# One key tile fewer summed on GpSimd: six of eight by additions, the last two by the ones product

## The reference

```python
result = embeddings @ w_qkv                       # 16 heads of 32
q, k, v = ...                                     # each (b, heads, s, 32)
scores = jnp.einsum('bnqd,bnkd->bnqk', q, k) / jnp.sqrt(jnp.float32(h))
probs = jax.nn.softmax(scores, axis=-1)
ctx = jnp.einsum('bnqk,bnkd->bnqd', probs, v)
...
x = _layernorm(x + attention(x))
x = _layernorm(x + ffn(x))
```

## Time and profile before

| | before |
|---|---|
| median of 3 runs | 4126.71 us (4125.9 to 4129.7) |
| the profiled execution, whole | 4124.68 us |
| its span, first to last instruction | 4123.0 us |
| PE busy | 3806.5 us, 92% |
| DVE busy | 3051.1 us, 74% |
| POOL busy | 2283.0 us, 55% |
| ACT busy | 1749.4 us, 42% |
| granted TensorE clock, mean | 0.977 |

### The profile page before, as it was taken

How to read it: one execution, slowest core, us unless ns; L and a number is a source line. 1 busy time by engine, 2 the same in 40 slices (tenths; PEclk the granted TensorE clock), 3 DMA queues, 4 the chain that set the end, 5 groups by cost and what they waited for, 6 DMA issues and landing times. The chain is left out here.

```text
span 4123.0 us, 61806 instructions
## 1 busy us (share of the span) xinstructions
PE 3806.5 (92%) x22985; PEld 1728.9 (42%) x22985; DVE 3051.1 (74%) x4929; ACT 1749.4 (42%) x3104; POOL 2283.0 (55%) x1446
## 2 busy tenths in 40 slices
PE   3489999999999999999999999999999999999999
PEld 2234344433543345433453434443454334534344
DVE  8866687676876778666786668776786667866787
ACT  3345522664235632455225552265423553245522
POOL 4468722885239832588227862298424883268722
PEclk9689999999999999999999999999999999999999
DMA  4110110111010110111101101101101111010110
GB/s 163 44 58 26 29 50 24 35 32 50 23 35 18 40 44 24 30 32 32 47 19 40 29 21 54 31 22 32 53 22 32 26 34 48 19 37 24 32 49 21
DMA packets 106560, 152.56 MB, mean 37 GB/s; under 512 B 28177, under 2 KB 55569, under 8 KB 106129
## 3 DMA queue, kind: packets, MB, share of 16 engines
q1 hardware_dynamic: 106256, 148.49, 11.6%
HBM read 76.28 MB, written 19.66 MB: 23 GB/s over the span
## 5 line engine op out<-in xcount | busy, mean ns | idle before, releaser
L571 DVE TENSOR_REDUCE mx<-R 128x1 f32<-128x512 f32 x2080 | 1334.4, 686 | 662.6 <-PE R L663 654.6
L1186 ACT ACTIVATE arena<-SC 128x512 f32<-128x512 f32 x1344 | 749.7, 603 | 413.9 <-PE SC L1438 411.0
L1512 PE MATMUL SC<-wgu,split 128*128 128x512 f16 (+1 forms) x3456 | 724.0, 364 | 0.6
L1084 POOL TENSOR_TENSOR wd<-wd,arena 128x1024 f32<-128x1024 f32 x208 | 485.7, 2357 | 31.0 <-ACT arena L1186 29.9
L1110 POOL TENSOR_TENSOR arena<-arena,sc_h 128x704 f32<-128x704 bf16 (+2 forms) x136 | 176.1, 1312 | 576.8 <-DVE arena L496 576.8
L1186 ACT ACTIVATE wd<-SC 128x512 f32<-128x512 f32 x704 | 399.8, 603 | 201.1 <-PE SC L1438 196.9
L1512 PEld LDWEIGHTS SC<-wgu,split 128*128 128x128 f16 x3456 | 338.3, 98 | 343.8 <-issue 12.6
L663 PE MATMUL R<-ks_even,qs_even 96*128 96x512 bf16 x1056 | 398.5, 399 | 88.6 <-issue 45.3
L1227 ACT ACTIVATE arena<-SC,gain 128x512 f32<-128x512 f32 (+1 forms) x192 | 125.1, 652 | 775.0 <-PE R L1512 390.7
L643 PE MATMUL R<-xT,wqkv 128*128 128x512 bf16 x1632 | 429.3, 386 | 11.4 <-DVE split L565 6.5
L663 PE MATMUL R<-arena 96*128 96x512 bf16 x1024 | 368.8, 382 | 17.6 <-DVE xT L558 11.6
(11 more groups left out here) (139 smaller groups left out, 5675.3 us busy)
## 6 DMA issues: line engine op xcount, KB each, us to landing
x<-n_L_attn_embeddings_dram SPq DMA_DIRECT2D x136, 256.0 KB, 2.9
wd<-wd_kept SPq DMA_DIRECT2D x32, 512.0 KB, 5.6
out_dram<-x SPq DMA_DIRECT2D x64, 256.0 KB, 2.0
ks_even<-split SPq DMA_DIRECT2D x204, 64.0 KB, 2.0
qs_even<-split SPq DMA_DIRECT2D x408, 32.0 KB, 1.8
arena<-split SPq DMA_DIRECT2D x192, 64.0 KB, 2.0
arena<-split SPq DMA_DIRECT2D x384, 32.0 KB, 1.8
wd<-wd_kept SPq DMA_DIRECT2D x16, 384.0 KB, 7.5
```

The source lines that it names most:

```text
L571: nc.vector.reduce_max(mx[:, j:j + 1], ring_of(ring, job)[:, :], AX_X).then_inc(max_done, 1)
L1084: nc.gpsimd.tensor_tensor(acc[u % 2][i], first, probs_of(s)[:, hs, :], ALU.add).then_inc(pool_sum, 1)
L1186: nc.scalar.activation(probs_of(s)[:, hd, :], SC[e % SLOTS][:, :], ACT.Exp, scale=SCALE).then_inc(exp_done, 1)
L1512: last = nc.tensor.matmul(GU[kk % 2][which][:, 0:w], xhT[i % 2][:, part_x * KH + k, :], wgu[:, part_w * KH + k, which * I + first:which * ...
```

## The change

One number of a table: the first seven units make five additions on POOL and not six. The last unit's four additions stay.

```diff
 QUARTERS = 4
-POOL_SUMS = [TILES - 2] * (UNITS - 1) + [TILES // 2]
+POOL_SUMS = [TILES - 3] * (UNITS - 1) + [TILES // 2]
```

## The result

The changed kernel takes **4206.76 us** (median of 4 runs, 4204.64 to 4207.3) against 4126.31 us for the kernel before in the same comparison: ratio **1.0192**, 95% interval 1.0175 to 1.021, 80.5 us slower. The forecast was 4201, 74 us slower.

What follows compares the result with a forecast made beforehand. PE was taken to bound the attention units, with POOL second and off the path. Products 49.3 plus waits 24.8 make 74 us, so 4201 against a median of 4126.71 (own band 4188 to 4214, range 4172 to 4232).

Steps and rivals of the forecast that it cites:

- Off the path and on it: In the attention units, the 264 us removed from POOL gain nothing, while the work added on PE lengthens the run.
- The product, 49.3 us: On PE, eight more matmul records per ones product cost 0.88 us in each of 7 units x 8 batches.
- The wait, 24.8 us: ACT's exponentials for tile 1 wait for the ones product to free tile 6's buffer; PE then waits, 3.10 us a batch.
- E: The start of PE's first matmul after the ones product, from which the forecast counts its times.
- The three kinds of unit: Loss by the wait: 0.67 us each in units 1 and 3, 0.41 in 2, 4 and 7, 0.53 in 5.
- the 0 of unit 6: In unit 6 three projection quarters stand among the matmuls, each due after what it waits for: loss 0.
- Rival D: New pauses in the attention units lower TensorE's clock: 1.75 us in each of 56 units, 98 us, 4299; chance 0.03.
- A: On PE, the products cost 49.3 us but later waits after tile 1 absorb the new ones: 4176; chance 0.13.
- B: PE's idle time in the units takes the new work in: 4127, or 4111 with gains; chance 0.06, half of it faster.
- C: The waits roll on through DVE, one 0.68 us operation late in six units: 33 us more, 4234; chance 0.10.
- The rule on the shared port: VectorE and GpSimd share an SBUF port lock, so fewer adds could free VectorE, at most 14 us; counted as nothing.

Runs made afterwards that it cites:

- e3: The kernel before, with GpSimd leaving out the tile 6 additions and nobody else adding that tile in the first seven units; 4125.15 us, ratio 0.9994.
- e9: e6 with the long ones product alone (tile 7 taken twice in the first seven units, six additions kept on GpSimd); 4146.75 us, +47.3 to e6.
- e10: e6 with the wait alone: ScalarE waits for the ones product, not the addition, before overwriting tile 6's buffer; 4130.10 us, +30.6 to e6.
- e7: The changed kernel with the projections of unit 6 made earlier, as in e6; 4175.31 us, +75.8 to e6.
- e6: The kernel before, with the projections of unit 6 made earlier (4, 4, 2, 2 quarters in steps 1 to 4); 4099.49 us, ratio 0.9936.
- e2: The kernel before, with one condition edited: ScalarE waits for the ones product, not the addition, before overwriting tile 6's buffer; 4161.10 us, ratio 1.0082.
- e1: The kernel before, with the ones product of the first seven units taking tile 7 twice (24 records), six additions kept on GpSimd; 4179.54 us, ratio 1.0128.

## Why the prediction was right

**Off the path and on it.** Right: POOL was busy 2018.8 us against 2019 forecast, and its 264 us were worth nothing (e3, -1.8 us with an interval across 0).

**The product, 49.3 us.** Right: 2.71 us from first record to the next matmul in units 1 and 2, where 2.74 was forecast; 0.85 x 56 = 48 us, and 47.3 measured in e9. The forecast's 0.88 was 0.02 to 0.03 too high.

**The wait, 24.8 us.** The mechanism and the order of the units are right, the size was too small; by the trace of the changed kernel it is 28 us, and by the units of e10 too. What failed is one term: ACT's first instruction behind the product was taken at E + 0.13, where the copy of the sums had started before. It starts at 0.22 (2260.03 - 2259.81), and the whole chain behind it, exponential, copy, DVE, is later by about that. The three kinds of unit, each with the matmul that the forecast names; unit 4 and unit 5 in the timeline of PE after:

```profile
2364.98 0.39 PE L1438 MATMUL SC<-qs_even,ks_even 98*128 98x512 bf16 x1
...
2368.53 0.39 PE L663 MATMUL R<-ks_even,qs_even 96*128 96x512 bf16 x1 [0.45 <-DVE split L565]
```

```profile
2401.01 0.66 PE L631 MATMUL R<-identf,x 128*128 128x128 f32 x4
...
2403.84 0.39 PE L1438 MATMUL SC<-qs_even,ks_even 98*128 98x512 bf16 x1 [0.59 <-ACT arena L1186]
2404.08 0.39 PE L663 MATMUL R<-arena 96*128 96x512 bf16 x1
```

| | forecast, after E | measured | before | loss forecast | loss measured |
|---|---|---|---|---|---|
| unit 1 (as 3) | 1.77 | 1.85 | 1.10 | 0.67 | 0.75 |
| unit 4 (as 2, 7) | 3.49 | 3.55 | 3.08 | 0.41 | 0.47 |
| unit 5 | 3.00 | 3.07 | 2.47 | 0.53 | 0.60 |

With these, 2 x 0.75 + 3 x 0.47 + 0.60 = 3.5 us a batch, 28 us in the run. The row of e10 in the table of units confirms them one by one, the units that are taken here as alike and the 0 of unit 6 included. Product and waits are then 76 us, and 75.8 is what e7 is above e6. That the forecast of the two together, 74, comes within 2 us of this is helped by a product put 1 us too high beside a wait put 3 us too low.

**The rest, 80.5 against 76.** Rival D, a lower clock behind the new pauses, is wrong as it was put: from the start of unit 1 to the end of unit 6 the granted clock of the fifth batch is 1.00 after the change, with all of its new pauses. What has changed is the clock in unit 7, behind the old wait on DMAs. Stretches of 37 us that begin there, of the fourth and the fifth batch (length, then busy time of the engines, then the granted clock); the kernel before, then after:

```profile
1930.00:1967.00 37.00, 32.57 (x237) 13.21 (x233) 26.66 (x45) 20.02 (x37) 24.30 (x15) 1.00 0.06 16
2417.00:2454.00 37.00, 33.94 (x233) 13.69 (x233) 26.66 (x45) 19.48 (x36) 22.56 (x14) 0.95 0.05 14
```

```profile
2252.00:2464.00 212.00, 203.41 (x1322) 79.22 (x1314) 143.35 (x241) 120.51 (x227) 147.06 (x67) 1.00 0.10 28
1970.00:2007.00 37.00, 33.71 (x223) 12.87 (x224) 25.21 (x42) 19.11 (x36) 20.89 (x12) 0.95 0.05 14
2467.00:2504.00 37.00, 34.42 (x239) 13.74 (x240) 26.10 (x43) 19.10 (x36) 21.07 (x13) 0.95 0.05 14
```

Before, the spell at the lower level (1.2 GHz) came in the fifth batch and not in the fourth; after, in both. Over all eight batches the granted clock of such a stretch is 0.91, 1.00, 0.95, 1.00, 0.95, 1.00, 0.95, 1.00 before and 0.95 in every one after. 0.05 x 37 = 1.9 us is the estimated price of one; in the kernel before, unit 7 up to the FFN lasts 32.75 us in the fourth batch and 34.49 in the fifth, 1.7 more. The lengths of the batches agree. The first matmul of batches 3 to 6, before and after:

```profile
1208.13 0.61 PE L663 MATMUL R<-ks_even,qs_even 96*128 96x512 bf16 x1 [6.13 <-issue]
1695.20 0.61 PE L663 MATMUL R<-ks_even,qs_even 96*128 96x512 bf16 x1 [6.54 <-issue]
2181.09 0.61 PE L663 MATMUL R<-ks_even,qs_even 96*128 96x512 bf16 x1 [6.55 <-issue]
2668.07 0.61 PE L663 MATMUL R<-ks_even,qs_even 96*128 96x512 bf16 x1 [6.48 <-issue]
```

```profile
1228.65 0.61 PE L663 MATMUL R<-ks_even,qs_even 96*128 96x512 bf16 x1 [5.94 <-issue]
1725.12 0.61 PE L663 MATMUL R<-ks_even,qs_even 96*128 96x512 bf16 x1 [6.14 <-issue]
2222.61 0.61 PE L663 MATMUL R<-ks_even,qs_even 96*128 96x512 bf16 x1 [6.46 <-issue]
2718.73 0.61 PE L663 MATMUL R<-ks_even,qs_even 96*128 96x512 bf16 x1 [6.45 <-issue]
```

The third batch takes 487.07 us before and 496.47 after, the fifth 486.98 and 496.12: 9.4 and 9.1 us more, and 9.3 was forecast. The fourth takes 485.89 and 497.49, 11.6 more: it is the one that had no such spell before. In e6 and e7 the wait is gone, and unit 7's clock is 1.00 in both batches in either of them. The units say where the rest is: in units 1 to 5 the change costs the same with the wait in unit 7 as without it, to 0.02 us; in units 6 and 7 of the eight batches together it costs 23.5 us in the two profiled executions with the wait, and 17.3 in those without. So the rest of 4 to 6 us lies around the wait on DMAs, which the change doesn't touch, and fits spells of lower clock behind it, met by more batches since the change moved them. The forecast had no term for it. The intervals of the ratios, some 7 us to either side, are too wide for the times alone to show it, and no run moved the spells by themselves, so the clock as the cause is read from the traces and not shown.

**The other rivals.** A (the later waits take the new ones in) falls by e2 and e10. B (PE's idle time takes the work in) falls by the result: PE's waits at the ends of units are as long after (0.49 and 0.57 us on ACT) as before, and the one on DMAs is still 3.27. C put 33 us more on DVE operations; DVE's lateness shows in PE's waits on its subtraction (L565), 15.8 us in 40 waits against 5.2 in 16, but it is part of the chain that the forecast counted: the waits cost 28 us in all, where C put 25 + 33.

**The rule on the shared port.** The Trainium skill, SBUF — State Buffer, section "SBUF: two separate sides", lets GpSimd block VectorE only where VectorE runs in one of its faster modes or reads two inputs from SBUF. The trace agrees as far as it goes: with 112 additions fewer the maxima, which read PSUM alone, last 656 to 694 ns in e3, 657 to 694 before. An instruction with two SBUF inputs beside an addition was not measured.

## What to carry to other kernels

An engine that is 55% busy and always in time gives nothing back when it is relieved; look at who waits for it, not at how busy it is. When a job changes hands, look for what its completion frees: here the buffer's release moved from an engine that was early to a job that stands behind the very work that needs the buffer, and more than a third of the price (28 of 76 us) was that wait. Such a chain can be worked out from a trace of before, step by step from the instruction that now ends last; here it came out within 0.1 us in each unit. And where the medians of whole runs are too coarse, compare one stretch, unit by unit: its length repeats from batch to batch to a hundredth of a us.

## What the runs showed of the hardware that I had not expected

Eight f32 matmuls into four column groups cost 0.85 to 0.88 us when they come among others, though each is recorded with 0.59 us. An exponential that waits for a matmul job starts 0.22 us after the matmul behind that job (2260.03 against 2259.81), a copy in the same place 0.13 (2217.75 against 2217.62). And a wait of 3.27 us on DMAs costs more than itself in some batches: the granted clock of the 37 us that begin with it is 0.91, 0.95 or 1.00, and which of them changes with edits elsewhere that leave the wait as it is (fifth batch: 0.95 before and after, 0.91 in e1; fourth: 1.00 before, 0.95 after).
